# A graph-attention kernel on one core: the first score tile moved ahead of the last count group, and the score tiles' pairs of PSUM banks swapped

## The reference

```
h = relu(layernorm(x))
q, k, v = h @ Wq + bq, h @ Wk + bk, h @ Wv + bv
adj[src, dst] = 1
a = q @ k.T / sqrt(512);  a = a * adj + (1 - adj) * -1e6
x = x + softmax(a) @ v

h = relu(layernorm(x));  h = agg(h @ W1 + b1)      # agg: sum over edges and loops, weights from degrees
h = agg(relu(batchnorm(h)) @ W2 + b2)
x = x + h
```

## Time and profile before

| what | value |
|---|---|
| timed, median of 3 runs | 311.57 us (311.39 to 311.7) |
| span of the profiled execution, first to last instruction | 309.8 us |
| PE busy | 295.1 us, 95% of the span |
| PE weight loads busy | 227.4 us, 73% |
| DVE busy | 210.2 us, 68% |
| ACT busy | 143.6 us, 46% |
| POOL busy | 55.4 us, 18% |
| mean DMA rate | 70 GB/s |

### The profile page before, as it was taken

The page is one execution under the profiler, slowest core; times in us unless marked ns, Lnnn a source line. Parts: engine busy times, 40 slices in busy tenths (PEclk is TensorE's granted clock), DMA queues, the critical chain, the costliest instruction groups (busy, mean ns, idle before and its releaser), DMA issues.

```text
span 309.8 us, 4740 instructions
## 1 busy us (share of the span) xinstructions
PE 295.1 (95%) x1319; PEld 227.4 (73%) x1319; DVE 210.2 (68%) x470; ACT 143.6 (46%) x245; POOL 55.4 (18%) x96
## 2 busy tenths in 40 slices
PE   2999969899999999999999999999999999999995
PEld 2977436565666688888888888888788888888884
DVE  3787999999997747667647575757444288376311
ACT  1799944443445626635465445437632035233000
POOL 5234280000000170032121212203010043100000
PEclk9999999999999999999999999999999999999999
DMA  7707040000420127832834636133203000000221
GB/s 268 291 3 204 1 135 0 3 0 0 150 57 3 33 36 107 200 85 53 136 69 102 135 46 124 36 68 59 44 0 70 1 0 2 0 0 2 101 103 68
DMA packets 42310, 21.65 MB, mean 70 GB/s; under 512 B 35760, under 2 KB 36016, under 8 KB 42288
## 3 DMA queue, kind: packets, MB, share of 16 engines
q1 hardware_dynamic: 41744, 20.33, 26.9%
q10 hardware_dynamic: 544, 1.05, 0.9%
HBM read 10.88 MB, written 2.10 MB: 42 GB/s over the span
## 4 chain that ended last, share of the span: by engine, by line
PE 79%; DVE 10%; issue 4%; DVEq 4%; DMA 1%; ACT 1%; SPq 0%; ACTq 0%
PE ps L948 18%; PE ps L950 18%; PE ps L949 18%; PE ps L1196 9%; PE ps L1119 8%; PE ps L1018 5%; DVE src_oh L668 4%; PE ps L986 2%; DVEq L668 2%; DVE dst_oh L670 2%; DMA edge_i<-src_in 1%; DVE hT L651 1%; DVEq L670 1%; DVEq L660 0%; DVEq L674 0%
## 5 line engine op out<-in xcount | busy, mean ns | idle before, releaser
L668 DVE TENSOR_SCALAR src_oh<-iota,ecol 128x512 f16 x149 | 44.2, 346 | 4.0 <-issue 2.9
L1018 PE MATMUL ps<-src_oh,dst_oh 128*128 x149 | 37.9, 382 | 5.4 <-DVE dst_oh L670 4.6
L1018 PEld LDWEIGHTS ps<-src_oh,dst_oh 128*128 x149 | 14.4, 103 | 25.6 <-issue 16.7
L1119 PE MATMUL ps<-cnt,qh 128*128 128x512 f32 x128 | 30.1, 391 | 0.3 <-ACT cnt L541 0.3
L1196 PE MATMUL ps<-qh,cnt 128*128 128x512 f32 x128 | 29.3, 390 | 0.0
L443 ACT ACTIVATE cnt<-ps 64x512 int16<-64x512 f32 x32 | 18.9, 592 | 20.7 <-PE ps L1032 20.3
L1119 PEld LDWEIGHTS ps<-cnt,qh 128*128 128x128 f32 x128 | 23.9, 188 | 5.6 <-DVE qh L827 0.7
L1196 PEld LDWEIGHTS ps<-qh,cnt 128*128 128x128 f32 x128 | 23.9, 188 | 5.2 <-DVE vb L929 0.3
L950 PE MATMUL ps<-v,pT 128*128 128x512 f32 x64 | 25.0, 390 | 0.0
L948 PE MATMUL ps<-v,pT 128*128 128x512 f32 x64 | 24.9, 390 | 0.0
L949 PE MATMUL ps<-v,pT 128*128 128x512 f32 x64 | 24.9, 390 | 0.0
(11 more groups left out here) (176 smaller groups left out, 658.8 us busy)
## 6 DMA issues: line engine op xcount, KB each, us to landing
xt<-x_in SPq DMA_DIRECT2D x16, 256.0 KB, 3.3
out<-xt SPq DMA_DIRECT2D x8, 256.0 KB, 2.1
qk_raw<-L_gnn_Wk_in ACTq DMA_DIRECT2D x2, 512.0 KB, 4.9
qk_raw<-L_gnn_Wq_in SPq DMA_DIRECT2D x2, 512.0 KB, 6.7
wB_raw<-L_gnn_Wv_in SPq DMA_DIRECT2D x2, 512.0 KB, 8.9
wB_raw<-L_gnn_W_in SPq DMA_DIRECT2D x2, 512.0 KB, 4.3
w_raw<-L_gnn_W_in SPq DMA_DIRECT2D x2, 512.0 KB, 4.8
bias_row<-L_gnn_b_in SPq DMA_DIRECT2D x2, 256.0 KB, 3.7
```

What stands on the lines that cost most here:

```text
L668: dve.tensor_scalar(src_oh[:, bass.ds(slot, 1), j, :].rearrange("p a n -> p (a n)"), iota[:, :], ecol[:, bass.ds(c + j, 1)], None, ALU.is_ ...
L1018: m = pe.matmul(ps[:, i % 2, :], dst_oh[:, bass.ds(slot, 1), :, j].rearrange("p a n -> p (a n)"), src_oh[:, bass.ds(slot, 1), j, :].rearra ...
L1119: m = pe.matmul(bank(g), qh[:, d, a, c * P:(c + 1) * P], cnt[:, d, n * HALF:(n + 1) * HALF], start=(d == 0 and a == 1), stop=last)
```

## The change

The first score tile, `scores(0)`, is now issued on PE ahead of `counts` of the last window, behind the item `w`; the other seven stay where they were. Windows still own banks 0 and 1 at that point, so the score tiles swap their pairs: even tiles now use banks 2 and 3, odd ones 0 and 1. The wait for `c16` at 32 goes from tile 0 to tile 1, and DVE's read at L768 names the swapped pair. Nothing is added or taken out.

```diff
@@ DVE, mask_and_max
             dve.copy_predicated(T[:, t % 2, :], adj[:, t % ADJ, :],
-                                ps[:, 2 * (t % 2):2 * (t % 2) + 2, :].rearrange("p a n -> p (a n)")
+                                ps[:, 2 * ((t + 1) % 2):2 * ((t + 1) % 2) + 2, :].rearrange("p a n -> p (a n)")
                                 ).then_inc(S["masked"], 1)
@@ PE, scores and its place
+        def scores(t):
+            if t == 0:
+                pe.wait_ge(S["item_lo"], nth(("q", 0, KC - 1)))
+            if t == 1:
+                pe.wait_ge(S["c16"], 2 * NW)
...
+                    m = three(bank(2 * ((t + 1) % 2) + n), lambda a: qh[:, t, a, k * P:(k + 1) * P],
...
+            if i == NW - 1:
+                scores(0)
             counts(i, now)
...
-            if t == 0:
-                pe.wait_ge(S["c16"], 2 * NW)
-                pe.wait_ge(S["item_lo"], nth(("q", 0, KC - 1)))
...
-                    m = three(bank(2 * (t % 2) + n), lambda a: qh[:, t, a, k * P:(k + 1) * P],
...
         for i in range(NT):
-            scores(i)
+            if i >= 1:
+                scores(i)
```

More of the change, by code:

```diff
@@ L1043, in _ @@
         bounds = bounds_of(0)
+        def scores(t):
[3 more added lines that the diff above has]
+                pe.wait_ge(S["c16"], 2 * NW)
+            if t == 4:
+                pe.wait_ge(S["item_lo"], len(items))
+            if t >= 2:
+                pe.wait_ge(S["masked"], t - 1)
+            for n in range(2):
+                for k in range(KC):
+                    m = three(bank(2 * ((t + 1) % 2) + n), lambda a: qh[:, t, a, k * P:(k + 1) * P],
+                              lambda a: hT[:, a, k, n * HALF:(n + 1) * HALF], k == 0, k == KC - 1)
+            m.then_inc(S["s_ps"], 1)
         for i in range(NW):
@@ L1057, in _ @@
         make(("q", 1, 0))
-        def scores(t):
-            if t == 0:
-                pe.wait_ge(S["c16"], 2 * NW)
-                pe.wait_ge(S["item_lo"], nth(("q", 0, KC - 1)))
[L1063 to L1068, removed]
-                    m = three(bank(2 * (t % 2) + n), lambda a: qh[:, t, a, k * P:(k + 1) * P],
-                              lambda a: hT[:, a, k, n * HALF:(n + 1) * HALF], k == 0, k == KC - 1)
-            m.then_inc(S["s_ps"], 1)
         def weighted_v(t):
```

## The result

The changed kernel is slower, and by more than forecast: median 313.56 us (312.73 to 314.81, 4 runs) against 311.48 us (311.33 to 311.70, 4 runs), ratio 1.0073 with a 95% interval of 1.0052 to 1.0094. The forecast was 312.5, its upper end 313.5.

The account below looks back on a forecast made before the run. PE, busy 295.1 of 309.8 us, was taken as the bound, with the strand from `adj` to `weighted_v(0)` deciding. PE's 1.05 us is given back and 0.9 us more lost: 311.57 + 0.9 = 312.5 us, range 311.5 to 313.5.

Parts of the forecast that it names:

- PE's own gain of 1.05 us: From item `w` to `weighted_v(0)`, PE's gaps at the last window go, so PE alone would arrive 1.05 us earlier.
- The last window 4.4 us later: The last window's closing matmul stands 6.98 us behind the start of item `w` instead of 2.59, 4.4 us later.
- Adj, not the scores, releases the first masking, and the strand to `pT` has no slack: Tile 0's masking waits for `adj` landing, not `scores(0)`; ACT and DVE work from there to `p_hi(0)` absorbs none of 0.9 us.
- Masking 0.9 us late: DVE's masking of tile 0 starts 0.9 us later: 4.4 us of delay less 3.5 us of slack; bounds 0.8 to 1.2.
- No fall of the clock: TensorE's clock stays at 1.00 through PE's expected idle time of some 1.9 us ahead of `weighted_v(0)`.
- The rival: TensorE's clock falls in PE's new idle time ahead of `weighted_v(0)`, costing up to 2.7 us: 314 to 315.2; chance 0.05.
- The swap of banks costs nothing: In the score tiles, swapping bank pairs costs nothing by itself: each tile still has two, reused after the same masking.
- No second wait behind it: After `weighted_v(0)` PE works without a gap; `weighted_v(1)` has 2.7 us in hand, so no second wait appears.

## Why the prediction was wrong

*PE's own gain of 1.05 us*: right. With 6 or 12 matmuls ahead, where nothing else is late, the kernel gains 1.0 us on the same stretch; in the changed kernel itself the last item's last matmul starts at 124.44, so PE is ready 23.6 us behind item `w`, as forecast.

*The last window 4.4 us later*: right; 7.04 - 2.59 = 4.45.

*Adj, not the scores, releases the first masking, and the strand to `pT` has no slack*: right. With zeros from a ready buffer the masking moved up by 0.96 us, and the gap shrank by 1.0. The 1.6 us by which the masking was late are the 1.6 us by which the span behind item `w` grew.

*Masking 0.9 us late*: the first step that was mis-sized. The landing was taken as 3.3 us, between 3.2 and 3.6, because "the first has an empty queue as before". The queue was not what mattered: the delayed window also brings POOL's work to within 0.3 us of the issue, and the landing is 3.8 us. That is 0.5 us of the missing 0.7; the rest is DVE starting 0.2 us behind the landing, not the 0.05 us assumed. The forecast for an execution whose clock holds would have been 311.5 + 1.6 = 313.1 with these two; 312.7 to 313.2 were measured.

*No fall of the clock*: the second, and the one that put the median out of the range. The rival was there with its place and its price (up to 2.7 us; measured 1.9), but with a chance of 0.05, by the reasoning that the clock had outlasted 2.6 us of idle time at the end of the span and the gap would be 1.9. Both halves failed. The gap was 2.3 us, and one observation of 2.6 us is no threshold: with 2.1 to 2.3 us the clock fell in 14 of 31 executions. The three traces that hold a fall show it when PE starts again or up to 0.6 us later, so the idle time up to a fall can't be read as the idle time that leads to one. The price, too, was read from a place that doesn't show it by its clock: the transposes at the start of the span take twice as long as later ones, but the profile of the kernel before grants the full clock there (columns as in rows 2):

```profile
8.00:9.00 1.00, 1.00 (x7) 0.86 (x6) 0.74 (x3) 0.74 (x2) 0.00 (x0) 1.00 1.04 385
```

What makes the transposes slow there, the rows don't say. The price is taken better from the three traces with a fall. The page "TensorE: Matmul & The Clock Gate" of the Trainium skill (section "HAM oscillation") has such a fall between bursts when PE waits, with a cost of half the stretch at the lower clock; the rows agree on the cost, 1.7 of 3.4 us. The waits that the page tells of are longer than the 1.9 us forecast and the 2.3 us measured, so by the page the clock would have held here; the measurement decides.

*Luck in the median*: where the clock holds, 312.7 to 313.2 us lie inside the range of 311.5 to 313.5, although the masking was 0.7 us later than forecast. Of four sets of the same kernel two have medians inside it (313.03, 312.99) and two outside (313.56, 314.7), by how many executions a fall had. The measured median is outside because of the fall, and the mis-sized landing alone would not have put it there. What decides whether a given execution has a fall is open.

*The swap of banks costs nothing*: right, 0.9999.

*No second wait behind it*: right. The trace has one idle time of PE from the item `w` to 200 us, the one of 2.33 us. The rule of the Trainium skill ("DMA: Bandwidth & Descriptors", section "Rules for kernel authors") on issuing a DMA early and waiting late, weighed in the prediction, holds in this sense: up to 12 matmuls could leave the stretch between the issue and the use for nothing, and those beyond 12 were paid for: 1.1 us for the next 6, another 1.2 for the last 6 in executions whose clock holds.

## What to carry to other kernels

Work moved ahead of a producer to fill a gap delays everything that hangs on the producer; measure the gap and the slack of what hangs on it, and move no more than the gap needs. Here 0.7 us of idle time needed 6 matmuls, and 24 turned a gain of 1.0 us into a loss of 1.4 or 3.3. And a new gap of 2 us on TensorE has two prices, its length and, in part of the executions, a stretch at the lower clock behind it; with few runs the median then says little, and the mean clock of each run says more.

## What the runs showed of the hardware

- The granted clock fell in 14 of 31 executions with a gap of 2.1 to 2.3 us on a busy TensorE, in 4 of 4 with 3.4 us, in 0 of 27 with 1.4 us or less. In the three traces that hold such a fall it begins at the gap's end or behind it (about 127.54 us with PE back at 127.54; about 128.1 with PE back at 127.56; about 129.0 with PE back at 128.41), lasts 3.4 us and so costs 1.7 us.
- A DMA transpose of a 128x1024 tile of 16-bit numbers from SBUF to SBUF lands in 3.3 us with GpSimd still (one trace) and in 3.8 us when GpSimd starts elementwise work (a power of 128x8, then adds of 128x512) 0.3 us behind its issue. When that work starts matters: 1.0 us behind the issue the landing is 3.6 us, 1.3 us behind it 3.3. The Trainium skill ("SBUF — State Buffer", section "SBUF: two separate sides") has the engines' ports and the DMAs' apart, with no contention between them; by that the landing should not depend on GpSimd, and here it does, by 0.5 us. Which part of the path the two share is open.
- A DVE subtraction of 128x1024 fp32 (L636) took 1.60 us in the one trace in which GpSimd's bias adds ran into its first 0.5 us, 1.22 us in those in which they had ended.
